# Filter stage: GpSimd instead of VectorE joins the last bank's products of a batch's second transform

## The reference

```
for n in range(ORDER):                       # ORDER = 2
    v_fft = jnp.fft.rfft(v, n=n_fft, axis=-1)      # n_fft = 2048
    h_fft = jnp.fft.rfft(h[n], n=n_fft, axis=-1)
    y = jnp.fft.irfft(v_fft * h_fft, n=n_fft, axis=-1)[..., :L]
    v = y * x[:, n]
return v.transpose(0, 2, 1) @ w_out.T + b_out
```

## Time and profile before

| | before |
|---|---|
| median of 3 runs | 683.04 us |
| the profiled execution | 682.95 us |
| its span | 681.0 us |
| TensorE matmul busy | 650.6 us (96%) |
| VectorE busy | 611.0 us (90%) |
| ScalarE busy | 384.5 us (56%) |
| GpSimd busy | 365.1 us (54%) |
| instructions | 12462 |

### The profile page before, as it was taken

How to read it: one execution, slowest core, us unless ns; L and a number is a source line. 1 busy time by engine, 2 the same in 40 slices (tenths; PEclk the granted TensorE clock), 3 DMA queues, 4 the chain that set the end, 5 groups by cost and what they waited for, 6 DMA issues and landing times. The chain is left out here.

```text
span 681.0 us, 12462 instructions
## 1 busy us (share of the span) xinstructions
PE 650.6 (96%) x4284; PEld 476.8 (70%) x4284; DVE 611.0 (90%) x1241; ACT 384.5 (56%) x761; POOL 365.1 (54%) x506
## 2 busy tenths in 40 slices
PE   9999999999999999999999999888999999999996
PEld 3588765788747887568887677556777775666664
DVE  4899887999999999999999979748999979999997
ACT  3742157131368503475222634569888886888885
POOL 0633424537235753258451381284577769788786
PEclk9999999999999999999999999999999999999999
DMA  8730055230453446443743057552222221010012
GB/s 310 204 63 1 0 125 105 81 62 7 66 107 69 93 155 62 93 93 63 200 100 87 1 185 98 213 174 80 64 80 79 79 79 33 1 34 32 32 63 94
DMA packets 52680, 60.73 MB, mean 89 GB/s; under 512 B 5416, under 2 KB 46376, under 8 KB 52362
## 3 DMA queue, kind: packets, MB, share of 16 engines
q1 hardware_dynamic: 43498, 40.28, 18.3%
q0 software_dynamic: 8256, 18.86, 16.7%
q10 hardware_dynamic: 864, 0.79, 0.4%
HBM read 33.72 MB, written 11.53 MB: 66 GB/s over the span
## 5 line engine op out<-in xcount | busy, mean ns | idle before, releaser
L747 ACT ACTIVATE yb<-banks 128x256 f32<-128x256 f32 x64 | 24.1, 385 | 137.5 <-PE banks L446 92.3
L437 PE MATMUL banks<-inv_m,spec_y 128*128 128x256 f32 x384 | 85.5, 379 | 0.0
L473 PE MATMUL banks<-xt_in,w_in 128*128 128x512 f32 x192 | 84.5, 594 | 0.2
L437 PEld LDWEIGHTS banks<-inv_m,spec_y 128*128 128x128 f32 x384 | 73.0, 190 | 9.9
L389 PE MATMUL banks<-z_cplx,fwd_m 128*128 128x256 f32 x240 | 71.9, 381 | 3.5 <-DVE prod L1172 3.2
L390 PE MATMUL banks<-z_cplx,fwd_m 128*128 128x256 f32 x240 | 71.4, 379 | 0.0
L473 PEld LDWEIGHTS banks<-xt_in,w_in 128*128 128x128 f32 x192 | 36.1, 190 | 43.0 <-issue 40.2
L389 PEld LDWEIGHTS banks<-z_cplx,fwd_m 128*128 128x128 f32 x240 | 44.9, 190 | 11.8 <-issue 5.2
L390 PEld LDWEIGHTS banks<-z_cplx,fwd_m 128*128 128x128 f32 x240 | 45.6, 190 | 6.2
L904 POOL TENSOR_TENSOR spec_y<-prod 128x256 f32<-128x256 f32 x35 | 25.4, 726 | 42.0 <-DVE prod L1172 41.2
L2203 DVE TENSOR_REDUCE peak<-ps_score 128x16 f32<-128x1024 f32 x32 | 38.9, 1215 | 8.7 <-PE ps_score L1668 8.7
(11 more groups left out here) (311 smaller groups left out, 1704.4 us busy)
## 6 DMA issues: line engine op xcount, KB each, us to landing
x_tok<-in_x SPq DMA_DIRECT2D x8, 512.0 KB, 4.3
x_tok<-in_b_out POOLq DMA_DIRECT2D x8, 512.0 KB, 13.9
inv_scratch<-inv_sum SPq DMA_DIRECT2D x16, 256.0 KB, 2.6
xa_t<-inv_scratch SPq DMA_DIRECT2D x16, 256.0 KB, 2.7
v_t<-left POOLq DMA_DIRECT2D x8, 511.5 KB, 5.2
x_t<-left POOLq DMA_DIRECT2D x8, 511.5 KB, 5.6
xt_in<-in_x_t SPq DMA_DIRECT2D x3, 1024.0 KB, 5.9
x_scratch<-x_tok SPq DMA_DIRECT2D x6, 512.0 KB, 4.1
```

Source lines behind the costliest of these rows:

```text
L437: last = mm(bank[:, odd * 2 * P:(odd + 1) * 2 * P], spec_y[:, j + odd, part * D + h * P:part * D + (h + 1) * P], inv_m[:, o:o + 2 * P], st ...
L473: last = mm(proj_pair(b, t)[:, c * 512:(c + 1) * 512], w_in[:, k, TILES[t] * P:(TILES[t] + 1) * P], xt_in[:, k, c * 512:(c + 1) * 512], st ...
```

## The change

For the first transform that a batch computes ahead for the next one (u + 2, whose products lie in `prod_in_v`), GpSimd's `add_products` now joins all eight banks instead of seven, and VectorE's `products` leaves out its two instructions for bank 7, with the wait on `prod_done` ahead of them. For the other transforms (products in `prod`) nothing changes. Six VectorE instructions go (three times L1176 and L1177) and six GpSimd instructions come; GpSimd signals `y_ready` for bank 7 there.

```diff
--- before.py
+++ after.py
@@ -895,8 +895,8 @@
-            def add_products(u, first=False, prod=prod):
-                for j in range(BANKS - 1):
+            def add_products(u, first=False, prod=prod, banks_of=BANKS - 1):
+                for j in range(banks_of):
                     pool.wait_ge(prod_done, 8 * u + j + 1)
                     if j == 0 and not first:
                         pool.wait_ge(inv_done, 8 * u)
@@ -1011,7 +1011,7 @@
                     if b:
                         norm_factors(b - 1)
                     turned_real_sums(u + 2)
-                    add_products(u + 2, prod=prod_in_v)
+                    add_products(u + 2, prod=prod_in_v, banks_of=BANKS)
                 add_bias(b)
                 gate_first(u + 1, (x1_even, x1_odd)[b % 2][:, 0, :], v_t[:, 0, :], None if last_one else 4 * (u + 3))
@@ -1171,7 +1171,7 @@
                     tt(prod[:, s, :].rearrange("p (c d) -> p c d", c=2), spectrum, re, ALU.mult)
                     tt(prod[:, s + 1, :].rearrange("p (c d) -> p c d", c=2), spectrum, im, ALU.mult)\
                         .then_inc(prod_done, 1)
-                    if j == BANKS - 1:
+                    if j == BANKS - 1 and prod is not prod_in_v:
                         dve.wait_ge(prod_done, 8 * (u + 1))
                         tt(spec_y[:, j, 0:D], prod[:, s, 0:D], prod[:, s + 1, D:2 * D], ALU.subtract)
                         tt(spec_y[:, j, D:2 * D], prod[:, s + 1, 0:D], prod[:, s, D:2 * D], ALU.add).then_inc(y_ready, 1)
```

## The result

The changed kernel took 685.24 us (median of 7 runs, 684.21 to 686.86); the kernel before, run beside it, took 683.43 us (7 runs, 682.29 to 683.61). By the medians it is 1.8 us slower, where 1.5 us were forecast. The ratio is 1.0032, 95% interval 1.0022 to 1.0041, which is 1.5 to 2.8 us. The profiled execution of the changed kernel has a span of 684.8 us and took 686.68 us; that of before has 681.0 and 682.95. This profile is thus 1.4 us above its own median, and part of what follows is to sort out what belongs to the change.

What follows compares the result with a forecast made beforehand. In the filter stage TensorE and VectorE were taken to run in turn, the later one at each meeting deciding. Rounds of 0.41 + 0.41 + 0.69 = 1.5 us on the median 683.04 gave 684.5 us, range 683.2 to 685.3.

Steps and rivals of the forecast that it cites:

- round 1: The edited instructions run three times, at the end of the products of batches 1 to 3; first at 166.6 us.
- the term of round 3, 0.69 us: TensorE's loads of the third complex bank start 0.69 us late in the last round, with nothing to hide it.
- The removal is worth 0.81 us only if nothing collides: Without VectorE's pair the rotations could start at T+0.60 instead of T+1.41: 0.81 us a round if nothing else holds them.
- The turns at the port: Rotations and GpSimd's added sums, both reading SBUF, alternate; L1193 starts at T+2.83, before at T+2.42: VectorE 0.41 us later.
- T: Start of VectorE's second product L1172 in each round; 165.90 in round 1 and 344.99 in round 3 before the change.
- two far places: L1072 against GpSimd's L915 and L923 after set-up; rotation L1186 against L939 near 416 us, 1.23 instead of 0.28 us.
- The rival without a collision: Short rotations slip in beside GpSimd's sums; VectorE gains 0.81 us in rounds 1 and 2; sum -1.0, 682.0 us; chance 0.12.
- The rival of a long hold: GpSimd keeps the port for both sums: 0.70 us in rounds 1 and 2, 0.6 in round 3; 685.0 us; chance 0.10.
- VectorE's shift of 0.41 us a round: In rounds 1 and 2 VectorE's rotations, and the matmuls it releases, come 0.41 us later, and the shift stays.
- The standstill, hidden in rounds 1 and 2: TensorE stands 0.6 us before the third complex bank, covered by its 1.01 us wait for L1207, shrinking to about 0.8.
- The rival in which the last batch absorbs all of it: Slack in the last batch's chain absorbs round 3's standstill; VectorE's shift alone counts, 3 x 0.41: 684.3 us; chance 0.15.
- Added waits and DMA issues at nothing: GpSimd's added wait costs nothing; L944's DMA issues and L939 come about 1.6 us later, with 4.09 us to spare.

Runs made afterwards that it cites:

- psum_after: The changed kernel with rotations taking input x from a PSUM bank, behind an added wait (rotations compute something else): 681.51 us, ratio 0.9987 to the kernel before.
- psum_before: The kernel before with rotations taking input x from a PSUM bank (rotations compute something else): 682.98 us, ratio 1.0003 to the kernel before.
- pad_after: The changed kernel with one more VectorE instruction per round, a long fulfilled wait ahead of the rotations: 685.18 us, ratio 1.0036 to the kernel before.
- first_two: The kernel before with the change in rounds 1 and 2 alone; VectorE keeps its pair in round 3: 684.27 us, ratio 1.0011.
- late_signal: The kernel before, VectorE keeping the pair, but GpSimd passes bank 7's signal to TensorE behind four small operations: 684.93 us, ratio 1.0022.
- only_third: The kernel before with the change in round 3 alone; VectorE keeps its pair in rounds 1 and 2: 683.81 us, ratio 1.0010.
- the second seven: Seven more runs of the same changed kernel file, nothing altered, against the kernel before (682.89 us): 685.85 us, ratio 1.0039.

## Where the prediction held, and where it failed

Two steps failed. The sum takes the removal as worth its own 0.81 us a round and nothing else, so it has no term for what six instructions less do to the rest of VectorE's stream; the runs show 0.36 us in round 1. And the term of round 3, 0.69 us, is the standstill in full; the runs show 0.49. Beyond the sum, the low clock that five of the changed kernel's fourteen runs have was put at nothing.

- **The removal is worth 0.81 us only if nothing collides.** Right. In psum_after L1231 starts 0.8 us earlier than its partner in psum_before; with the 0.11 us for which it is then held, 0.71 us are left in rounds 1 and 2.
- **The turns at the port.** Right in place, size and order: L1186 0.42, L1187 and L1189 0.81 us, forecast 0.4 and some 0.8; L1193 at T+2.82, forecast T+2.83; GpSimd's end T+2.34, forecast T+2.37. What the working read at two far places carried over to a pair of short instructions. The rival without a collision is excluded by these rows. Its sum of -1.0 us is what psum_after, where nothing collides with the rotations, measured in its three rounds (-0.99). The rival of a long hold (0.70 us in each of rounds 1 and 2) is excluded by the 0.39 us that pad_after and first_two show where the stall is absent. Its 685.0 us came nearer to the measured time than the forecast's 684.5, by coincidence.
- **VectorE's shift of 0.41 us a round.** Right: 0.44 and 0.39 us in round 2 of the changed kernel and of first_two, 0.39 us in round 1 of pad_after.
- **The standstill, hidden in rounds 1 and 2.** Right, and late_signal shows it alone. The wait of L446 was forecast to shrink to 0.8 us; it was 0.98 us in round 2. TensorE ends its projection of round 1 only 0.45 us later and not 0.6 (170.35 against 169.69 us, less the 0.21 us by which the whole trace is later at that point). In round 1 the wait was 1.33 us, through the stall of L1229.
- **Failed in size: round 3, 0.69 us.** The mechanism was right. The size was 0.49 us, and 0.48 alone. The load came 348.83 - 346.75 - 1.44 = 0.64 us late, 1.44 being the shift of all engines by then. The second load follows the first after 0.11 us instead of 0.216, so that 0.11 us are made up at once; the loads behind it keep their 0.216 us. Another 0.1 us is made up near 393 us, where TensorE waits for VectorE's L1172, in the kernel before and then in the changed one:

```profile
392.79 0.45 PE L389 MATMUL banks<-z_cplx,fwd_m 128*128 128x256 f32 x1 [0.73 <-DVE prod L1172]
394.67 0.45 PE L389 MATMUL banks<-z_cplx,fwd_m 128*128 128x256 f32 x1 [0.63 <-DVE prod L1172]
```

  The prediction's account of the last batch doesn't name this wait. Some 0.05 us are lost again by 400 us. The rival in which the last batch absorbs all of it (0.0) is excluded by late_signal and only_third.
- **Added waits and DMA issues at nothing.** Right: L944 starts 1.5 us later, and no view has anything that waits for it.
- **Failed: a term that the sum doesn't have.** 0.36 us in round 1, behind L1193. No row of the kernel before shows it, and it goes with one instruction more. The list of parts (what is removed, added and moved) had nothing for it: taking instructions out of a stream can bring a stall at a place that the edit doesn't touch. Why it does is open.
- **The clock.** It was said ahead of the prediction to play no part, from one profile of the kernel before. In the changed kernel's fourteen runs it does. The nine without the low clock have a median of 684.70 us, 1.7 us above the 682.96 of the kernel before's 35 beside them, which is what the rounds cost; with all fourteen it is 685.3.

The forecast sum, 0.41 + 0.41 + 0.69 = 1.5, measured as 0.41 + 0.44 + 0.49 and 0.36 for the stall, is 1.7 us. So two errors of opposite sign, +0.36 and -0.20, nearly cancelled: that the sum came out so close is in part luck. They moved the cost from 1.5 us, near the 1.37 us that the prediction took as the least change that can be told from none, to 1.7. The direction held. The range, 683.2 to 685.3, held by 0.06 us in the first seven runs, and the median of the second seven, 685.85, lies above it.

## What to carry to other kernels

In this kernel two instructions taken off VectorE and given to GpSimd were worth their time only where what VectorE ran next had at most one input in SBUF. With two, the engines took turns, and three rotations of 0.28 us took 0.42, 0.81 and 0.81 us, 1.2 us more, where the removal gave 0.81. So look at the instructions behind the one that is moved, and put work with a PSUM input there. And where a few tenths of a microsecond decide, subtract the starts of the same instructions in both traces, stretch by stretch, ahead of and behind each edit, and don't trust the difference of two spans.

## What the runs showed of the hardware that I had not expected

**The granted clock of TensorE falls in some executions, at the same place.** In the first profile of the changed kernel it fell from full speed (2.4 GHz) to half (1.2 GHz) at about 470.5 us and came back at 474 us; in the kernel before it did not. The view by windows, before and then changed (us, busy time and count of PE, PEld, DVE, ACT, POOL; granted clock; DMA share; GB/s):

```profile
465.00:470.00 5.00, 3.39 (x67) 2.79 (x69) 4.08 (x4) 4.59 (x9) 2.44 (x2) 1.00 0.37 108
470.00:475.00 5.00, 5.00 (x72) 3.69 (x60) 4.43 (x7) 4.71 (x9) 3.25 (x2) 1.00 0.18 52
```

```profile
465.00:470.00 5.00, 3.39 (x61) 2.29 (x54) 3.41 (x4) 4.60 (x9) 3.59 (x2) 1.00 0.20 58
470.00:475.00 5.00, 5.00 (x72) 3.62 (x72) 3.40 (x3) 4.88 (x9) 3.43 (x2) 0.66 0.18 50
```

TensorE had been busy 3.39 of the 5 us ahead of it in both. It cost 1.6 us of the 1.8 us behind 400 us. only_third shows the same fall at about 469 us (0.90 in the window to 470 us, 0.76 in the one from there), which is the same place in the program once the shifts are taken off, and the same 1.6 us; the other twelve profiles don't. The two profiles with the fall are also the only two of the fourteen whose mean granted clock is 0.996, where the others have 0.997 to 0.999. If that mark is taken for the fall, the runs that have no profile can be counted too: 5 of 14 of the changed kernel, 2 of 5 of pad_after, 2 of 12 of first_two, 2 of 11 of only_third, 2 of 9 of late_signal, 1 of 11 of psum_after (683.98 us, where its median is 681.51), but none of 67 of the six other kernels, and 4 of 101 of the kernel before. In the changed kernel's second set the two runs at 0.999 took 683.62 and 683.90 us, the three at 0.996 took 686.24 to 686.85 us. So the fall was more frequent with the change than without it, too much so for chance to be likely, and it is part of why the medians differ by more than the rounds cost. How the change brings it about isn't shown.

**An idle time of VectorE of 0.36 us whose place moves** with how many instructions stand ahead of it (pad_after, above).

**Behind a standstill TensorE's second weight load follows the first after 0.11 us,** against 0.216 us between loads before and after it. The same 0.11 us stands behind the 0.6 us of the changed kernel and behind the 1.1 us of late_signal.
